# Audio attention: the weighted averages head by head in 32-column tiles of the tensor engine, and the four heads of a window picked by one ACT operation

## The chip, the cores and the metric

The program runs on one core of a Trainium2 chip. The metric is the device time of one execution in microseconds; lower is better. Times are medians over runs; rows of a trace come from one profiled execution. The engines are called PE (TensorE products), PEld (TensorE weight loads), DVE (VectorE), ACT (ScalarE), POOL (GpSimd) and SP (SyncE, whose queue issues the DMAs).

## The reference, cut to what matters

Two layers of cross attention and an MLP work on x (8 batches x 56 queries x 256), and then a second block lets the same queries attend to the 1500 rows of "audio". The change lies in that second block:

```python
B, Tt, D = hidden_states.shape        # 8, 56, 256; 16 heads of 16 columns
a = _layer_norm(audio_kv, ln_gamma, ln_beta)            # 8 x 1500 x 256
Q = (hidden_states @ Wq.T).reshape(B, Tt, HEADS, HEAD_DIM).transpose(0, 2, 1, 3)
K = (a @ Wk.T).reshape(B, Ta, HEADS, HEAD_DIM).transpose(0, 2, 1, 3)
V = (a @ Wv.T).reshape(B, Ta, HEADS, HEAD_DIM).transpose(0, 2, 1, 3)
scores = jnp.einsum('bhtd,bhsd->bhts', Q, K) * scale    # masked
attn = jax.nn.softmax(scores, axis=-1)
out = jnp.einsum('bhts,bhsd->bhtd', attn, V)            # the averages
out = out.transpose(0, 2, 1, 3).reshape(B, Tt, D) @ Wo.T
return hidden_states + jnp.tanh(gate) * out
```

## The kernel before, in words

Everything is f16 in two parts: a number is a high part plus a low part, and a product of two such numbers is two or three f16 products. A program of five queues without barriers, one for each engine, runs through the layers; semaphores are its only order.

**The two layers and the MLP** take the first 1147 us. The change doesn't touch them.

**The audio attention** works on tiles of 128 rows. For one batch the 16 heads x 56 queries are 896 rows, seven tiles (RT = 7), 56 tiles in all, numbered y; b is the batch and s the tile in it. Heads stand in four windows of four (HW = 4, NW = 4); a window is WR = 224 rows. Each head has 2 x 16 = 32 columns in the values, the high and the low half side by side (2 * KA = 32), so a window is 128 columns wide. For one tile:

- PE `audio_scores` forms 128 x 1536 scores in three banks of PSUM, 6 products where the tile touches one window and 12 where it touches two; it waits until DVE has read the scores of the tile before (`as_max`), since there is one set of banks.
- DVE `audio_minimum` (L1538) adds the mask and finds the extreme; ACT `audio_exponentiate` (L1286) takes the exponential; DVE `audio_scale` (L1545, L1547) forms the inverse sum; ACT `audio_high` (L1295) writes the high part of the probabilities, DVE `audio_low` (L1556) the low part.
- SP `turn_audio` (L555, L557) transposes high and low part by DMA into `probT`, 24 pieces (2 x NT, NT = 12) of up to 128 audio rows each.
- Between them PE forms `unit`s, the values and keys of the next batch (twelve a batch, 6 products of 512 columns each), which ACT (L1279) and DVE (L1597) split into high and low part, and SP (L546) transposes the keys.

**The averages.** Four times a batch PE runs `audio_average(b, w)` for a window: for high and low part of the probabilities, over 12 pieces of the audio rows, it loads 128 columns of values (four heads) and streams the window's 224 rows of `probT`. The bank then holds, for each head's 32 partitions, all four heads' queries, of which only the diagonal blocks of 32 x 56 are wanted. ACT `pick_average` takes these with four activations (L1303), adds a bias and writes `attnT`. PE may not overwrite the bank before that (`attn_ready`, two averages back).

The order is written out by hand: `SLOT_WINDOWS` says at which tile PE runs which window's average (tiles 1, 2, 4 and 6 of a batch; the last two windows in the batch after), `SLOT_PICKS` at which tile ACT picks it (0, 2, 3 and 5), `SLOT_UNITS` where the units stand. In PE's order a tile is: scores, one unit, an average if there is one, another unit. In ACT's: the high part of the tile before, units, a pick if there is one, the exponential. The last batch has no units. At the very end the last two windows of batch 7 are averaged, picked, multiplied with the output weights (f32, 56 columns, L769 SC<-small,ctxT) and written out.

L769 is the helper `mm` through which every product goes; groups of it are told apart by their tiles: SC<-qc are audio scores, SC<-ctxT units, PV<-core with 224 columns the averages of the change.

Of the kernel before, what the change touches and what calls it, by code (L numbers as in the profile page):

```python
# [18 lines left out]
ACT = mybir.ActivationFunctionType  # L19
# [6 lines left out]
B, Q, D, T, H, F = 8, 56, 256, 1500, 16, 1024  # L26
# [5 lines left out]
NT = -(-T // P)  # L32
# [11 lines left out]
KA = D // H  # L44
HW = 4
NW = H // HW
WR = HW * Q
# [15 lines left out]
PROB_SCALE = 4096.0  # L63
# [31 lines left out]
def build(nc, x_t, ctx_nat, ctx_t, ctx_p, mask, pack, vrows, gate, wq, wk, wv, wo, wkv2, wq2, wo2, w1, w2, scratch, out):  # L95
    es = ExitStack()
    with es:
        def sb(name, shape, dt=F32):
            return es.enter_context(nc.sbuf_tensor(name, shape, dt))

        def sem(name):
            return es.enter_context(nc.semaphore(name))
# [40 lines left out]
        probT = arena.bitcast(F16).rearrange("p (x r) -> p x r", x=2 * NT)  # L143
# [69 lines left out]
        attnT = small[:, 0:NW * NQ].rearrange("p (w n) -> p w n", w=NW)  # L213
        hm = sb("hm", [P, HW])
        vbias = sb("vbias", [P, NW])
# [5 lines left out]
        PV = [es.enter_context(nc.psum_tensor(f"PV{i}", [P, 512], F32)) for i in range(2)]  # L221
# [31 lines left out]
        attn_ready = sem("attn_ready")  # L253
# [168 lines left out]
        def values(n, w):  # L422

            v = n % VSLOTS * UNIT
            return core16[:, v + w * P:v + (w + 1) * P]
# [5 lines left out]
        def col(name, c):  # L431
            a = PACK[name] + c
            return pk[:, a:a + 1]
# [13 lines left out]
        def width(c):  # L447

            return LAST if c == NT - 1 else P
# [317 lines left out]
        def _(pe):  # L767
            def mm(o, a, c, start, stop, skip=False):
                return nc.tensor.matmul(o, a, c, start=start, stop=stop, skip_group_check=skip)  # L769
# [223 lines left out]
            def audio_average(b, w):  # L993

                n = NW * b + w
                y = RT * b + FIRST_TILE[w]
                if n >= 2:
                    pe.wait_ge(attn_ready, n - 1)
                if w == 0:
                    pe.wait_ge(m_lo, NT * (b + 1))  # L1000
                for i in range(2):
                    for k in range(2):
                        pe.wait_ge((apth_full, aptl_full)[i][k], 16 * ((y + 2 - k) // 2))
                    for j in range(NT):
                        r = width(j)
                        ins = mm(PV[w % 2][:, 0:WR], values(NT * b + j, w)[0:r, :],
                                 probT[0:r, i * NT + j, w * WR:(w + 1) * WR], j == 0 and i == 0, j == NT - 1 and i == 1)
                ins.then_inc(apv_done, 1)

            def audio_attention():  # L1010

                for y in range(RT * B + 3):
                    if y < RT * B:
                        audio_scores(y)
                    for n in slot_units(y)[0:1]:
                        unit(n, y)
                    if at_slot(SLOT_WINDOWS, y):
                        audio_average(*at_slot(SLOT_WINDOWS, y))
                    for n in slot_units(y)[1:]:
                        unit(n, y)  # L1020
                    if y == RT * B:
                        for m in range(DC):
                            early_output(m)
# [124 lines left out]
            for w in range(NW):  # L1148
                for c in range(DC):
                    pe.wait_ge(x_ready, 2 * DC + c + 1)  # L1150
                    ins = mm(banks[w][:, 0:NQ], wqa[:, c, w, :], xT[:, c, :], c == 0, c == DC - 1)
# [3 lines left out]
            for w in range(NW):  # L1155
                pe.wait_ge(attn_ready, NW * (B - 1) + w + 1)
                for m in range(DC):
                    ins = mm((M, S[0])[m][:, 0:Q], woa[:, w, m * P:(m + 1) * P], attnT[:, w, EARLY:NQ], w == 0, w == NW - 1)
# [5 lines left out]
        def _(act):  # L1164
# [132 lines left out]
            def pick_average(b, w):  # L1297

                n = NW * b + w
                act.wait_ge(apv_done, n + 1)  # L1300
                for h in range(HW):
                    own = slice(2 * KA * h, 2 * KA * (h + 1))
                    ins = nc.scalar.activation(attnT[own, w, b * Q:(b + 1) * Q], PV[w % 2][own, h * Q:(h + 1) * Q],  # L1303
                                               ACT.Identity, scale=1.0 / PROB_SCALE, bias=vbias[own, w:w + 1])
                ins.then_inc(attn_ready, 1)

            def mask_row(b, par):

# [10 lines left out]
            def audio_attention():  # L1319

                for y in range(RT * B + 4):
                    b, s = divmod(y, RT)
                    if 0 < y <= RT * B:
                        audio_high(y - 1)
                    for n in slot_units(y - 1)[1:]:
                        unit_high(n, y)
                    if at_slot(SLOT_PICKS, y):
                        pick_average(*at_slot(SLOT_PICKS, y))
                    if b < B:
                        audio_exponentiate(y)  # L1330
                    for n in slot_units(y)[0:1]:
                        unit_high(n, y)
                    if s == 3 and b + 1 < B:
                        mask_row(b + 1, (b + 1) % 2)
                    if s == 5 and b + 1 < B:
                        mask_addend(b + 1, (b + 1) % 2)
# [43 lines left out]
            for f in range(FC):  # L1380
                act.wait_ge(f1_mm, f + 1)
                if f >= 2:
                    act.wait_ge(f1_lo, f - 1)
                nc.scalar.activation(hid[:, f % 2, :], TB[f % 2][:, 0:NQ], ACT.Gelu, scale=1.0 / W_SCALE,
                                     bias=col("b_fc1", f)).then_inc(f1_act, 1)
# [473 lines left out]
```

## Time and profile before

| | |
|---|---|
| median of 3 runs | 1471.31 us (1470.87 to 1472.1) |
| the profiled execution: its time, its span | 1475.24 us, 1473.2 us |
| busy share: PE, PEld, DVE, ACT, POOL | 96%, 61%, 67%, 59%, 32% |
| instructions | 24729 |
| averages of the audio attention | 32, of 24 products of 224 columns |
| picks | 32, of 4 activations of 32x56 |

The span runs from the first to the last instruction; the execution's own time is a little longer. Busy time of products counts from the start of one to its modelled end, and products overlap, so two neighbouring starts say more than a mean duration. The chain that ended last is followed back from the last instruction, at each step to what released it.

### The profile page before, as it was taken

What the parts mean: (1) busy time and instruction counts of PE and PEld (TensorE: products, weight loads), DVE (VectorE), ACT (ScalarE), POOL (GpSimd) and SP (SyncE); (2) the same over time, 40 slices, a digit from 0 to 9 for tenths busy, and PEclk for the clock granted to TensorE, in tenths of its full rate; (3) what the DMA queues carried; (4) which work ended last, traced back from release to release, by engine and by line L of the source; (5) the groups of instructions that cost most, each with busy time, mean ns of one, the idle gap of its engine ahead of it and who ended that gap; (6) DMA issues with size and microseconds to landing.
All of it is one profiled execution on the core that took longest, in us unless ns stands there. A gap on an engine that the chain in (4) does not pass through costs nothing.

```text
span 1473.2 us, 24729 instructions
## 1 busy us (share of the span) xinstructions
PE 1417.8 (96%) x9188; PEld 891.8 (61%) x9188; DVE 985.8 (67%) x2034; ACT 868.5 (59%) x1566; POOL 471.0 (32%) x379
## 2 busy tenths in 40 slices
PE   9999999999999899999999999999999999999987
PEld 5466666666666554466666666666554454555545
DVE  6765555555555557766666566665556888888886
ACT  5744554455445447555445544554445788889896
POOL 3545334334334200234432523420011333334300
PEclk9999999999999999999999999999999999999999
DMA  6299899888888730599989989887722799999998
GB/s 207 78 227 192 164 183 184 175 173 179 179 172 182 150 97 29 115 207 182 190 161 185 182 165 181 179 165 147 180 51 50 136 210 211 220 214 223 215 199 164
DMA packets 672083, 246.95 MB, mean 168 GB/s; under 512 B 644716, under 2 KB 646236, under 8 KB 671964
## 3 DMA queue, kind: packets, MB, share of 16 engines
q1 hardware_dynamic: 671964, 245.38, 82.4%
q8 instruction: 73, 1.20, 0.4%
q14 instruction: 46, 0.38, 0.1%
HBM read 85.28 MB, written 0.52 MB: 58 GB/s over the span
## 4 chain that ended last, share of the span: by engine, by line
PE 71%; DVE 9%; ACT 7%; DMA 6%; issue 3%; SPq 2%; ACTq 0%; DVEq 0%
PE SC L769 38%; PE PV L769 33%; DMA core<-qc 3%; DVE qc L1556 2%; ACT qc L1295 2%; DVE core L1597 2%; DMA core<-core 2%; DVE prob L1538 2%; DMA qc<-core 2%; ACT prob L1286 1%; ACT core L1279 1%; ACT small L1303 1%; DVE core L1589 1%; SPq L515 1%; SPq L557 0%
## 5 line engine op out<-in xcount | busy, mean ns | idle before, releaser
L769 PE MATMUL PV<-core 128*128 128x256 f16 (+1 forms) x4800 | 540.5, 270 | 17.3 <-DMA core<-qc 5.6
L769 PEld LDWEIGHTS PV<-core 128*128 128x128 f16 x4800 | 458.4, 98 | 87.5 <-issue 13.7
L1228 ACT ACTIVATE prob<-SC,core 128x500 f32<-128x500 f32 x336 | 223.7, 674 | 413.0 <-DVE core L1562 413.0
L769 PE MATMUL SC<-ctxT,qc 128*128 128x500 f16 x2016 | 443.7, 374 | 0.0
L1531 DVE TENSOR_REDUCE mx<-SC 128x1 f32<-128x500 f32 x336 | 224.4, 669 | 322.5 <-PE SC L769 322.5
L769 PEld LDWEIGHTS SC<-ctxT,qc 128*128 128x128 f16 x2016 | 196.0, 97 | 206.8
L697 POOL CAST ctxT<-stage 128x750 f16<-128x750 f32 x64 | 68.9, 1076 | 446.7 <-PE SC L769 235.5
L1589 DVE SCALAR_TENSOR_TENSOR core<-prob,core 128x1500 f16<-128x1500 f32 x112 | 194.6, 1738 | 4.1 <-ACT core L1237 4.0
L1237 ACT ACTIVATE core<-prob 128x1500 f16<-128x1500 f32 x112 | 162.7, 1453 | 3.5
L769 PE MATMUL SC<-ctxT 128*128 128x512 f16 x576 | 136.9, 381 | 9.1 <-DVE core L1597 8.9
L769 PE MATMUL SC<-qc 128*128 128x512 f16 x480 | 112.7, 379 | 13.0 <-DVE mx L1538 13.0
L701 POOL TENSOR_TENSOR core<-stage,core 128x768 f16<-128x768 f32 x64 | 110.9, 1733 | 9.8 <-DVE core L1437 4.8
L701 POOL TENSOR_TENSOR ctxT<-stage,ctxT 128x750 f16<-128x750 f32 x64 | 102.6, 1604 | 12.8 <-DVE core L1437 8.0
L1556 DVE SCALAR_TENSOR_TENSOR qc<-prob,rsc,qc 128x1500 f16<-128x1500 f32 x56 | 100.2, 1788 | 9.2 <-ACT qc L1295 9.0
L769 PEld LDWEIGHTS SC<-ctxT 128*128 128x128 f16 x576 | 55.5, 98 | 77.2 <-DVE core L1597 12.4
L1538 DVE CUSTOM_DVE_ANT_0 prob<-SC,rowbuf 128x1500 f32<-128x1500 f32 x56 | 95.9, 1712 | 9.1 <-PE SC L769 9.1
L1295 ACT ACTIVATE qc<-prob,rsc 128x1500 f16<-128x1500 f32 x56 | 86.2, 1540 | 22.3 <-DMA core<-qc 14.0
L719 POOL CAST ctxT<-stage 128x768 f16<-128x768 f32 x32 | 26.8, 839 | 219.6 <-PE SC L769 147.9
L697 POOL CAST core<-stage 128x768 f16<-128x768 f32 x64 | 55.1, 860 | 130.6 <-DMA stage<-in_ctx_nat_dram 129.1
L1597 DVE SCALAR_TENSOR_TENSOR core<-SC,rstd,core 128x256 f16<-128x256 f32 x192 | 83.5, 477 | 19.3 <-ACT core L1279 19.2
L1286 ACT ACTIVATE prob<-prob,mx 128x1500 f32<-128x1500 f32 x56 | 86.4, 1544 | 13.7 <-DVE mx L1538 12.9
L769 PEld LDWEIGHTS SC<-qc 128*128 128x128 f16 x480 | 45.8, 97 | 68.8 <-issue 18.7
(134 smaller groups left out, 1329.0 us busy)
## 6 DMA issues: line engine op xcount, KB each, us to landing
stage<-in_ctx_nat_dram SPq DMA_DIRECT2D x64, 384.0 KB, 4.0
stage<-in_ctx_t_dram SPq DMA_DIRECT2D x64, 375.0 KB, 3.4
stage<-in_ctx_p_dram SPq DMA_DIRECT2D x32, 384.0 KB, 3.9
core<-in_wq_dram SPq DMA_DIRECT2D x8, 512.0 KB, 4.0
core<-in_wk_dram SPq DMA_DIRECT2D x8, 512.0 KB, 3.6
core<-in_wv_dram SPq DMA_DIRECT2D x8, 512.0 KB, 5.2
core<-in_wo_dram SPq DMA_DIRECT2D x8, 512.0 KB, 5.0
core<-core SPq DMA_TRANSPOSE x224, 4.2
```

The lines of the kernel that those rows point to most:

```text
L697: nc.gpsimd.tensor_copy(hi, src).then_inc(split_hi, 1)
L701: nc.gpsimd.tensor_tensor(lo, src, hi, ALU.subtract).then_inc(stage_free, 1)
L769: return nc.tensor.matmul(o, a, c, start=start, stop=stop, skip_group_check=skip)
L1228: nc.scalar.activation(prob[:, i, c * CW:c * CW + w], SETS[i][c][:, 0:w], ACT.Exp, bias=nmax[:, i, :], accum_out=sum3[:, i, c:c + 1]).then ...
L1237: nc.scalar.activation(ph[:, i, 0:T], prob[:, i, 0:T], ACT.Copy, scale=UP).then_inc(ph_hi, 1)
L1286: nc.scalar.activation(prob[:, i, 0:T], prob[:, i, 0:T], ACT.Exp, scale=-1.0, bias=mx3[:, i, 0:1], accum_out=sum3[:, i, 0:1]).then_inc(as_ ...
L1295: nc.scalar.activation(aph[:, i, 0:T], prob[:, i, 0:T], ACT.Copy, scale=rsc[:, y % 4, 1:2]).then_inc(aph_hi, 1)
L1531: nc.vector.tensor_reduce(mx3[:, t % 2, c:c + 1], SETS[t % 2][c][:, 0:w], AX_X, ALU.max)\
L1538: nc.vector.tensor_tensor_reduce(out=prob[:, i, 0:T], in0=scores_of(y), in1=maskb[:, b % 2, :], scale=1.0, scalar=3.0e38, op0=ALU.add, op1 ...
L1556: nc.vector.scalar_tensor_tensor(aph[:, i, TC:TC + T], prob[:, i, 0:T], rsc[:, y % 4, 1:2], aph[:, i, 0:T], ALU.mult, ALU.subtract).then_i ...
L1589: nc.vector.scalar_tensor_tensor(ph[:, i, TC:TC + T], prob[:, i, 0:T], UP, ph[:, i, 0:T], ALU.mult, ALU.subtract).then_inc(ph_lo, 1)
L1597: ins = nc.vector.scalar_tensor_tensor(lo[:, i, :, :], src[:, i, :, :], rstd[:, n:n + 1], hi[:, i, :, :], ALU.mult, ALU.subtract)
```

## The change

Each of the 24 steps of an average becomes four: for head h the 32 columns of its values are loaded, the 56 rows of its own queries are streamed, and the result goes to the head's own 32 partitions of the bank, in columns 0 to 55. An average is then 96 loads of 32 columns and 96 products of 56 columns. The bank holds the wanted blocks only, side by side in the partitions, so ACT picks a window with one activation of 128x56.

```diff
                     for j in range(NT):
                         r = width(j)
-                        ins = mm(PV[w % 2][:, 0:WR], values(NT * b + j, w)[0:r, :],
-                                 probT[0:r, i * NT + j, w * WR:(w + 1) * WR], j == 0 and i == 0, j == NT - 1 and i == 1)
+                        v = values(NT * b + j, w)
+                        for h in range(HW):
+                            own = slice(2 * KA * h, 2 * KA * (h + 1))
+                            c = w * WR + h * Q
+                            ins = mm(PV[w % 2][own, 0:Q], v[0:r, own], probT[0:r, i * NT + j, c:c + Q],
+                                     j == 0 and i == 0, j == NT - 1 and i == 1)
                 ins.then_inc(apv_done, 1)
...
                 act.wait_ge(apv_done, n + 1)
-                for h in range(HW):
-                    own = slice(2 * KA * h, 2 * KA * (h + 1))
-                    ins = nc.scalar.activation(attnT[own, w, b * Q:(b + 1) * Q], PV[w % 2][own, h * Q:(h + 1) * Q],
-                                               ACT.Identity, scale=1.0 / PROB_SCALE, bias=vbias[own, w:w + 1])
-                ins.then_inc(attn_ready, 1)
+                nc.scalar.activation(attnT[:, w, b * Q:(b + 1) * Q], PV[w % 2][:, 0:Q], ACT.Identity,
+                                     scale=1.0 / PROB_SCALE, bias=vbias[:, w:w + 1]).then_inc(attn_ready, 1)
```

## Rows read from the trace of the kernel before

**Rows 1.** The page: the chain that ended last, by engine.
```profile
PE 71%; DVE 9%; ACT 7%; DMA 6%; issue 3%; SPq 2%; ACTq 0%; DVEq 0%
```

**Rows 2.** The chain by line, cut to 1184.4 to 1426 us, then to 1426 to 1473.2.
```profile
by line: DMA core<-qc 15.9%; issue 12.7%; DVE qc L1556 10.0%; DMA qc<-core 9.7%; ACT qc L1295 9.0%; PE SC L769 7.6%; DVE core L1597 6.4%; ACT core L1279 5.2%; ACT prob L1286 5.1%; DVE prob L1538 5.1%; PE PV L769 3.5%; ACT small L1303 3.2%; 
...
by line: ACT qc L1295 12.9%; DVE qc L1556 11.1%; ACT prob L1286 10.5%; PE SC L769 9.5%; SPq L557 9.4%; issue 9.0%; DMA core<-qc 8.7%; SPq L555 6.8%; ACT small L1303 6.5%; DVE prob L1538 5.1%; PE PV L769 2.8%; DVE rsc L1545 1.5%; DVE rsc L15
```

**Rows 3.** us of the stretch, busy PE, PEld, DVE, ACT, POOL; PE clock, DMA share, GB/s.
```profile
1184.40:1225.80 41.40, 38.58 (x230) 21.62 (x229) 35.78 (x64) 36.13 (x53) 15.44 (x12) 1.00 1.09 214
...
1348.60:1390.00 41.40, 38.82 (x230) 21.70 (x229) 36.98 (x66) 37.41 (x55) 15.43 (x12) 1.00 1.13 214
```

**Rows 4.** Timeline of PE: start, us, what, count; a batch in its middle.
```profile
1277.30 1.46 PE L769 MATMUL SC<-qc 128*128 128x512 f16 x6
1278.59 1.46 PE L769 MATMUL SC<-ctxT 128*128 128x512 f16 x6
1279.89 2.47 PE L769 MATMUL PV<-core 128*128 128x224 f16 x24
1282.20 1.03 PE L769 MATMUL SC<-ctxT 128*128 128x512 f16 x4
```

**Rows 5.** Waits, 1184.4 to 1390 us: total us, times, longest.
```profile
ACT qc L1295 <- DMA core<-qc: 12.5, 8, 2.7
...
DVE prob L1538 <- PE SC L769: 6.7, 9, 1.8
...
PE PV L769 <- issue: 4.1, 3, 2.0
```

**Rows 6.** The chain in order of time, first pieces of two picks.
```profile
1439.09 0.30 ACT small L1303
...
1443.97 0.30 ACT small L1303
```

**Rows 7.** Groups by shape on ACT, by name: the pick and its neighbours in size.
```profile
L1303 ACT ACTIVATE small<-PV,vbias x128: 282/298/303, 1175.4 to 1469.7; 32x56 f32<-32x56 f32 x128
...
L1209 ACT ACTIVATE small<-SC x2: 532/532/532, 60.7 to 600.7; 32x448 f16<-32x448 f32 x2
...
L1342 ACT ACTIVATE small<-small x2: 558/558/558, 508.0 to 1047.5; 128x448 f16<-128x448 f32 x2
```

**Rows 8.** Timelines of PE and PEld where products are small.
```profile
308.85 0.17 PE L769 MATMUL SC<-one,rowbuf 128*128 128x1 f16 x1
308.88 4.09 PE L769 MATMUL PV<-core 128*128 128x256 f16 x36
...
1086.73 1.84 PE L769 MATMUL SC<-pk,prob 128*128 128x1 f32 x16
1088.43 0.92 PE L769 MATMUL PV<-prob,core 128*128 128x448 f16 x4
...
1468.49 1.42 PEld L769 LDWEIGHTS SC<-small,ctxT 128*128 128x128 f32 x12
```

**Rows 9.** Timeline of PE where the width changes to 32 and back.
```profile
25.82 1.30 PE L769 MATMUL SC<-prob,core 128*128 128x448 f16 x6
26.95 1.30 PE L769 MATMUL SC<-core 128*128 128x448 f16 x6
28.18 0.93 PE L769 MATMUL SC<-prob,core 128*32 128x448 f16 x4
29.04 1.31 PE L769 MATMUL PV<-prob,core 128*128 128x448 f16 x6
```

**Rows 10.** Timeline of the last 20 us.
```profile
1453.70 1.46 PE L769 MATMUL SC<-qc 128*128 128x512 f16 x6 [1.91 <-DVE mx L1538]
...
1467.44 1.31 PE L769 MATMUL PV<-core 128*128 128x224 f16 x12 [0.48 <-DMA core<-qc]
...
1468.59 2.13 PE L769 MATMUL SC<-small,ctxT 128*128 128x56 f32 x16
1468.79 1.23 ACT L1303 ACTIVATE small<-PV,vbias 32x56 f32<-32x56 f32 x4 [2.47 <-PE PV L769]
```

## The prediction

> **What bounds the kernel now.** I read the page first: the tensor engine is busy 96% of the span (the table above) and holds 71% of the chain that ended last [rows 1]. That is an average over stages, so the second view is the chain cut to the stage that the change touches, the audio attention from about 1147 us on. There TensorE no longer leads: between 1184 and 1426 us its lines hold 7.6% and 3.5% of the chain, the DMA transposes 15.9% and 9.7%, DVE and ACT most of the rest [rows 2]. The third view, busy time by batch, shows why: in a batch of seven tiles TensorE is busy some 93% of the time, DVE and ACT 86 to 90%, DMA all of it, and the granted clock is 1.00 of 2.4 GHz [rows 3]. Busy is not occupied for TensorE, so I count: a batch issues 60 + 72 products of 512 columns, six of which take 1.29 us (1277.30 to 1278.59), and four averages of 2.31 us (1279.89 to 1282.20) [rows 4]. That is 132 x 0.215 + 4 x 2.31 = 37.6 us, against a mean batch of 41.1 us (five batches from 1184.4 to 1390.0, the first and the last in [rows 3]). TensorE has 3.5 us of room in a batch, 0.88 us for each average. The waits say where that room lies: in front of the averages (4.1 us of "issue", which I take for transposes still under way), while ACT waits 12.5 us for the same transposes to free its buffer [rows 5]. Last I read the stretch without units of keys and values (1426 us on): there ACT holds the chain, with three whole picks of four activations (1430.5, 1439.1, 1444.0), and L1303 alone has 6.5% [rows 2, 6].
>
> **The change, part by part.**
>
> The pick. Four activations of 32x56 take 1.23 us together, 0.30 us each [rows 7, 10]. One activation of 128x56 stands nowhere in the trace. From the nearest rows, 32x448 takes 532 ns and 128x448 558 ns, so four times the partitions cost at most 26 ns [rows 7]; I take 0.31 us, with 0.30 and 0.33 as ends. 32 picks save 0.92 us each: 29 us of ACT, most of it not on the chain.
>
> The average. 24 loads of 128 columns with products of 224 columns become 96 loads of 32 columns with products of 56: the same columns stream, in four times as many instructions. Before, 24 pairs take 2.31 us, 96 ns a pair, and the weight load is hidden behind the product. After, the product needs 96/4 = 24 ns, so whatever a small pair costs beside that decides. No row has such a pair. From below: if nothing else limited, 24 ns. From above: if a pair keeps today's pace whatever its size, 96 ns. Nearest rows: a product of one column is followed by the next pair after 0.03 us (308.85 to 308.88), so one pair can pass in 30 ns [rows 8]; sixteen loads of 128 f32 columns, each with a product of one column, take 1.70 us, 106 ns each, so 32 columns at that rate load in 26.5 ns; twelve such loads with 56-column products take (1.42 - 0.19)/11 = 112 ns each, so load and product overlap even when the product is short [rows 8]. I take 28 ns a pair, between 26.5 and 30: 96 x 0.028 = 2.69 us.
>
> To this comes the change of the array's shape. The trace has it: six full products of 448 columns take 1.13 us to the next group, but 1.23 us when the next group is 32 columns wide, and the four narrow ones then take 0.86 us to the next full one where 4 x 0.188 = 0.75 us would do [rows 9]. That is 0.10 us in and 0.11 us out, 0.21 us for each average. Its two halves have the same shape, so nothing is lost between them. Sum: 2.69 + 0.21 = 2.90 us against 2.31, +0.59 us an average, +2.4 us a batch. TensorE then needs 40.0 of 41.1 us: it still fits, barely.
>
> What it comes to. Between 1184 and 1426 us L1303 is 3.2% of a chain of 241.6 us, 7.7 us; a quarter of it remains, so 5.8 us go at most. Other chains run close beside it (DVE, transposes), so I count half, -2.9 us. The averages are 3.5%, 8.5 us; a quarter more is +2.1 us at first order, and 28 x 0.59 = 16 us if every average before the last batch's were on the path [rows 2]. In the last batch TensorE idles some 2 us before its scores [rows 10], so a longer average hides there, while the three picks on the chain give 3 x 0.92 = 2.8 us, of which I keep 2.3, since the transposes queued on SP from 1455 us on follow ACT only in part [rows 2, 6]. The end: the last half average starts at 1467.44, when its transpose lands, and takes twelve pairs, 1.15 us; 48 x 0.028 = 1.34 us plus the shape change in front of the closing products make +0.2 us, and the last pick gives -0.92 us, with the output products behind it [rows 10]. Sum: -2.9 + 2.1 - 2.3 - 0.7 = -3.8 us.
>
> The profiled execution took 1475.2 us for a span of 1473.2, 3.9 us above the median of 1471.3. A difference read in it is taken off the median: 1467.5 us. Without the cover named for the averages it is +14 us instead of +2.1, which is 1479 us.
>
> No DMA, no wait and no order on any queue changes, and ACT reads the same values from the bank as before. The instructions grow by 32 x 2 x 72 = 4608; against 24729 now, which I cost at nothing: the loads of a batch's averages are spread over 41 us.
>
> **The rivals.**
>
> *The four column tiles work at once.* Each head's weights sit in their own 32 columns; if a load and a product in one tile need not wait for those in the next, four pairs pass in 28 ns, 7 ns a pair, 0.67 + 0.21 = 0.9 us an average; half-way, at 14 ns, 1.6 us. TensorE gives 0.7 to 1.4 us back four times a batch. For it: nothing in the rows speaks against; the narrow products there all use one tile [rows 9]. Against: every load in the rows waits for its turn behind the one before. The chain's 8.5 us of averages shrink by 0.3 to 0.6 of them, -2.6 to -5 us in place of +2.1. With -2.9, -2.3 and -0.9 from the picks that is -10 us; DVE waits 6.7 us for scores in five batches [rows 5], of which I let 2 go: 1459 us, ends 1451 and 1465.
> The Trainium skill, TensorEngine Tiling (Array Packing), Key Properties, states that different tiles can load and multiply in parallel; by it this rival is the outcome. No row here has two tiles, so it is not shown.
>
> *A small pair costs more than 31 ns* (the other side). From 0.88 us of room, (2.31 + 0.88 - 0.21)/96 = 31 ns is where TensorE becomes the bound of every batch. If a load into a narrow tile does not overlap with the product before it, the pair is 26.5 + 24 = 50 ns, an average 5.0 us, +2.7 us, +10.8 us a batch: TensorE needs 48.4 us, with 1 us of waits 49.4, 8.3 us more than now, over about seven batches +58 us, less 5 us for the picks: 1525 us. At 35 ns it is about 1484 us; at today's 96 ns, 9.4 us an average, it would be some 180 us. For it: the 56-column pairs in the rows were never quicker than 112 ns, though of four times the columns and another type. Against: the 30 ns of one pair.
> The Trainium skill, TensorE: Matmul & The Clock Gate, Back-to-back issue gap, gives about 62 ns a MATMUL when it is decoded in microcode, and about 25 ns as the floor otherwise; by the first an average is 6.2 us and the time near 1555 us, by the second my 28 ns stand. The pair of 30 ns speaks for the second, but it is one pair and not ninety-six.
>
> *Nothing moves*: the DMA transposes (25.6% of the chain) pace the batches, and ACT's relief turns into waiting for them. Time: the end alone gives -3.0 us, the averages give that back: 1471 us. For it: that share, and ACT's 12.5 us of waits for them [rows 2, 5]. Against: the picks in the last batch, which no transpose covers [rows 6].
>
> **How the numbers follow.** A measurement of this kernel tells a change from none beyond 0.2%, 2.9 us. Serial pairs of 24 to 31 ns, my case: 0.34, at 1467.5 us, range 1460 to 1478; of it 0.23 is faster, 0.05 same, 0.06 slower. Nothing moves: 0.07, at 1471, all of it same. Tiles at once: 0.32, at 1459; 0.30 faster, 0.02 same. Dear pairs: 0.27, at 1525, from 1476 up; 0.26 slower, 0.01 same. Together faster 0.53, same 0.15, slower 0.32. The range reaches down to 1453 (0.05 lies below) and up to 1500, which takes in pairs up to some 40 ns and leaves 0.14 above.
>
> **What would show it.** PV<-core with 128x56 products, x3072 in place of 768; the 96 of one average, start to start, take 2.7 us plus 0.2: about 1.6 or 0.9 means tiles at once, 5 dear pairs. The pick as one activation of 128x56, x32, near 0.30 us. A batch still 40 to 42 us, with ACT down to some 80%. In the last stretch, picks follow one another at 4.0 us where it was 4.9 (1439.1 to 1444.0) [rows 6]. The granted clock stays full. I am wrong if the pair is over 31 ns, if the clock falls in the averages, or if the batches shorten by more than 1.5 us.

## The result, and the profile after

The changed kernel takes 1483.2 us (1481.2 to 1483.9, four runs); the kernel before took 1471.7 beside it. The ratio is 1.0071, 95% interval 1.0056 to 1.0086: 0.7% slower, where I had forecast 0.25% faster. It lies inside the range, on the wrong side.

The parts that the change names came out better than my central case. First the timeline of PE around one average, the pick, and the shapes of the averages (groups by shape, whole trace), against [rows 4, 7]:

```profile
1272.52 1.46 PE L769 MATMUL SC<-ctxT 128*128 128x512 f16 x6
1273.91 1.02 PE L769 MATMUL PV<-core 128*32 128x56 f16 x96
1275.22 1.46 PE L769 MATMUL SC<-qc 128*128 128x512 f16 x6 [0.28 <-DVE mx L1539]
```
```profile
L1305 ACT ACTIVATE small<-PV,vbias x32: 286/288/307, 1172.5 to 1475.5; 128x56 f32<-128x56 f32 x32
```
```profile
L769 PE MATMUL PV<-core 128*32 128x56 f16 x2816 | 34.0, 194 | 42.7 <-DMA core<-qc 31.9 <-issue 8.9 <-DVE core L1598 1.7
```

96 pairs of load and product take 1.02 us, 10.6 ns a pair, where 24 pairs took 2.31 us. (The 1.02 us hold the 0.19 us of the last product; from start to start a pair takes 8.3 ns.) The 56 columns of one product alone need 24 ns by the pace of the wide ones, so the four tiles do work at once. The four activations became one of 0.29 us. TensorE and ACT should have gained. But PE now stands idle 42.7 us before its averages, 31.9 of them for the DMA transposes of the probabilities. Before, the same row was

```profile
L769 PE MATMUL PV<-core 128*128 128x224 f16 x704 | 77.5, 261 | 9.8 <-DMA core<-qc 5.6 <-issue 4.1
```

The windows of five batches (same columns as [rows 3]; each from the first tile's minimum to the next batch's) say what that adds up to:

```profile
1183.00:1225.80 42.80, 35.05 (x518) 16.61 (x517) 35.88 (x64) 32.31 (x41) 15.44 (x12) 0.96 1.16 212
...
1352.00:1399.30 47.30, 35.66 (x518) 16.78 (x517) 36.00 (x63) 34.70 (x43) 15.42 (x12) 0.93 1.14 203
sum 216.30, PE 175.19 PEld 82.66 DVE 179.14 ACT 163.91 POOL 77.17; mean PE 35.04 PEld 16.53 DVE 35.83 ACT 32.78 POOL 15.43
```

PE's busy time of a batch fell from 38.6 to 35.0 us and ACT's from some 36 to 32.8, and yet the five batches take 216.3 us in place of 205.6. (The batch behind them took 34.4 us in place of 37.3, so 2.9 us of these 10.7 came back.) The DMA share stays at its full value. The whole stage, from the first minimum on DVE to the last, before and then after (xcount, shortest/median/longest, first and last start):

```profile
L1538 DVE CUSTOM_DVE_ANT_0 prob<-SC,rowbuf x56: 1707/1710/1721, 1148.9 to 1455.7; 128x1500 f32<-128x1500 f32 x56
```
```profile
L1539 DVE CUSTOM_DVE_ANT_0 prob<-SC,rowbuf x56: 1706/1710/1722, 1146.0 to 1460.5; 128x1500 f32<-128x1500 f32 x56
```

That is 306.8 us before and 314.5 after: 7.7 us lost in the stage. From the last minimum to the end of the span it is 17.5 us and 20.8: 3.3 us more. Together 11.0 of the 11.5 us. (The two spans differ by 8.1 us only, because the stage began 2.9 us earlier in the trace after. The layers in front of it are untouched, and in the traces of the experiments it begins anywhere from 1145.1 to 1149.0 us, whichever averages the kernel has; only e9's begins later.)

The waits from 1184.4 to 1397 us answer to [rows 5], the chain by line to [rows 2] (1184.4 to 1426 us, then 1426 to the end):

```profile
ACT qc L1299 <- DMA core<-qc: 30.4, 16, 2.9
PEld PV L769 <- issue: 28.6, 25, 2.6
PE PV L769 <- DMA core<-qc: 23.0, 18, 3.5
```
```profile
by line: DMA core<-qc 25.2%; DMA qc<-core 10.6%; DVE qc L1557 9.4%; PE SC L769 9.0%; issue 8.3%; ACT qc L1299 7.1%; SPq L555 4.6%; SPq L557 4.3%; DVE core L1598 4.0%; DVE prob L1539 3.4%; ACT core L1283 3.3%; ACT prob L1290 2.5%; SPq L485 1
...
by line: SPq L555 38.0%; SPq L557 27.1%; DMA core<-qc 9.3%; PE SC L769 6.5%; issue 4.9%; DVE prob L1539 3.1%; ACT qc L1299 2.6%; ACT rowbuf L1317 2.6%; PE PV L769 1.4%; ACT prob L1290 1.1%; DVE xT L1675 0.5%; SPq L554 0.3%; DVE mx L1539 0.0
```

The transposes' share of the chain grew from 25.6 to 35.8%, and in the last batch the chain runs on SP's queue, from one issue of a transpose to the next. So the transposes pace the stage, and they became slower. The DMA view of 1184 to 1430 us shows that, before and after (packets, MB and busy share per queue: q1 carries the data, q8 TensorE's instructions, q14 GpSimd's; last, a transpose's median us from issue to landing):

```profile
DMA packets 176670, 52.64 MB, mean 214 GB/s; under 512 B 173323, under 2 KB 174091, under 8 KB 176651
...
q1 hardware_dynamic: 176651, 52.40, 112.4%
q8 instruction: 11, 0.18, 0.4%
...
core<-qc SPq DMA_TRANSPOSE x87, 4.1
```
```profile
DMA packets 169727, 51.11 MB, mean 208 GB/s; under 512 B 166367, under 2 KB 167135, under 8 KB 169695
...
q1 hardware_dynamic: 169695, 50.65, 115.3%
q8 instruction: 24, 0.39, 0.6%
...
core<-qc SPq DMA_TRANSPOSE x83, 4.9
```

Only one line counts more work: q8, blocks of 16 KB of instructions, 24 in place of 11. The 4608 instructions that the change adds are, by the page's own blocks (91 against 73, 1.49 MB against 1.20), 18 blocks more. Those hardly count by their bytes. They count by what happens around them. The same view over 4 us around one such block, before (1225 to 1229 us) and after (1210 to 1214), in 40 slices of 0.1 us:

```profile
DMA  9999999999999999999999000000000100000399
GB/s 225 212 207 207 205 228 212 215 218 174 141 174 182 241 259 412 220 218 187 105 20 3 0 0 0 0 0 0 0 5 8 10 8 10 10 10 8 77 292 289
```
```profile
DMA  9999999999999999190000001000005999999999
GB/s 154 174 246 287 294 289 289 292 292 292 267 287 282 435 276 154 36 20 0 0 0 0 3 8 10 8 10 10 10 10 113 284 292 297 289 289 289 294 292 500
```

For 1.7 and 1.4 us all data traffic of the core stops; 8 to 10 GB/s is the block itself. It is the same in both kernels, only over twice as often after. Counted from the packets of 1190 to 1420 us, stretches of at least 0.4 us under 60 GB/s add up to 16.6 us before and 34.3 after; 10.9 and 29.4 us of that lie at q8 blocks. After, 20 of the 22 blocks of this stretch have such a stop (before, 7 of 10); it lasts 1.0 to 2.0 us, median 1.4, and begins some 0.4 us behind the block's first packet. Part is caught up: behind the stop the queue moves some 290 GB/s.

The transposes feel it one by one. From 1184 to 1430 us, those that had a q8 block in flight between their issue and their landing landed after a median of 5.5 us before (23 of them) and 5.6 after (35); those that had none landed after 4.1 us in both kernels (63 and 26; the trace records no landing for the rest), and none of these took over 5.2 us. So a single transpose is not slower for the change; more of them meet a block.

Could TensorE instead be waiting for its own instructions? After, its idle stretches of over 0.2 us from 1184 to 1430 us add up to 45.2 us; 0.5 us of it ended while a block was being fetched or within 0.6 us behind it. Of the 8.7 us that PE waits for "issue" before averages, 8.1 end within 0.25 us of a transpose's landing.

At the end the granted clock is the other thing that changed. Two windows of after, the second from the closing products on, and PE's last row, against [rows 10]:

```profile
1470.00:1475.40 5.40, 2.11 (x145) 1.79 (x144) 0.00 (x0) 0.31 (x1) 0.00 (x0) 0.50 1.08 191
1475.40:1481.30 5.90, 3.64 (x20) 3.46 (x16) 0.55 (x2) 0.31 (x1) 0.00 (x0) 0.50 0.05 10
```
```profile
1475.37 3.66 PE L769 MATMUL SC<-small,ctxT 128*128 128x56 f32 x16
```

The closing products run at a granted clock of 0.50, the 1.2 GHz level, 3.66 us where 2.13 stood; TensorE had waited for the last transposes before them.

### The profile page after: what moved, and what is told of

It is laid out like the page before. It is cut to its first block, busy times and chain, and to the rows that moved or that the text cites. A ratio compares the mean times of both kernels' runs of the same rounds, so it can differ in the third digit from the quotient of the medians.

```text
span 1481.3 us, 29241 instructions
## 1 busy us (share of the span) xinstructions
PE 1386.8 (94%) x11492; PEld 850.4 (57%) x11492; DVE 983.5 (66%) x2034; ACT 837.3 (57%) x1470; POOL 472.1 (32%) x379
## 3 DMA queue, kind: packets, MB, share of 16 engines
q8 instruction: 91, 1.49, 0.4%
## 4 chain that ended last, share of the span: by engine, by line
PE 71%; DMA 8%; DVE 8%; SPq 6%; ACT 5%; issue 2%; ACTq 0%; DVEq 0%
PE SC L769 38%; PE PV L769 32%; DMA core<-qc 5%; SPq L555 2%; DVE qc L1557 2%; DMA qc<-core 2%; SPq L557 2%; DMA core<-core 2%; ACT qc L1299 1%; DVE core L1598 1%; DVE prob L1539 1%; ACT core L1283 1%; ACT prob L1290 1%; DVE core L1590 1%; SPq L485 1%
## 5 line engine op out<-in xcount | busy, mean ns | idle before, releaser
L769 PE MATMUL PV<-core 128*128 128x256 f16 (+1 forms) x7104 | 494.5, 238 | 49.8 <-DMA core<-qc 31.9
L769 PEld LDWEIGHTS PV<-core 128*128 128x128 f16 (+1 forms) x7104 | 415.6, 97 | 124.6 <-issue 40.2
L769 PE MATMUL SC<-ctxT 128*128 128x512 f16 x576 | 140.9, 389 | 9.2 <-DVE core L1598 9.1
L769 PE MATMUL SC<-qc 128*128 128x512 f16 x480 | 118.1, 391 | 20.1 <-DVE mx L1539 17.3
L1557 DVE SCALAR_TENSOR_TENSOR qc<-prob,rsc,qc 128x1500 f16<-128x1500 f32 x56 | 100.2, 1788 | 16.2 <-ACT qc L1299 11.0
L701 POOL TENSOR_TENSOR ctxT<-stage,ctxT 128x750 f16<-128x750 f32 x64 | 102.6, 1604 | 12.8 <-DVE core L1438 8.0
L769 PEld LDWEIGHTS SC<-qc 128*128 128x128 f16 x480 | 46.0, 100 | 81.9 <-issue 36.5
```

The lines of the kernel that those rows point to most:

```text
L701: nc.gpsimd.tensor_tensor(lo, src, hi, ALU.subtract).then_inc(stage_free, 1)
L1557: nc.vector.scalar_tensor_tensor(aph[:, i, TC:TC + T], prob[:, i, 0:T], rsc[:, y % 4, 1:2], aph[:, i, 0:T], ALU.mult, ALU.subtract).then_i ...
```

## The experiments

Theories named in the expectations: A, the transposes pace the stage, so what ACT or TensorE saves turns into waits; B, the loss is the clock that falls when TensorE idles between its shorter averages; C, it is TensorE coming early, so that its units and scores press on the other queues. From e5 on: F, the fetched blocks of TensorE instructions; G and G', the tiles themselves, or the SBUF reads of their loads, disturb the DMA engines; H is C again. Ratios are to the kernel before, run beside the experiment. "Blocks" are q8 blocks from 1184 to 1430 us, 11 before and 24 after. Where work is left out, the expectation says which.

**e1, tiles alone.** The pick with four activations, as before, on the new layout:

```python
for h in range(HW):
    own = slice(2 * KA * h, 2 * KA * (h + 1))
    ins = nc.scalar.activation(attnT[own, w, b * Q:(b + 1) * Q], PV[w % 2][own, 0:Q], ...)
```

> The averages as 32-column tiles, but each window still picked by four ACT operations of 32x56. Theory A (the queue of DMA transposes on SP sets the pace of the audio stage, so that what ACT or TensorE saves turns into waits): the time is that of the changed kernel, 1481 to 1486 us, since ACT's 0.93 us a pick were on no path. Rival (ACT's relief gives something and the tiles cost all of it): 1486 to 1500 us, as 32 x 0.93 = 30 us of ACT work come back.

1485.3 us, 1.0086 (1.0069 to 1.0102), 23 blocks from 1184 to 1430 us. The whole loss comes with the tiles.

**e2, the pick alone.** The averages as before, one activation of 128x56.

> The averages as before (128 columns, 224 rows), each window picked by one ACT operation of 128x56; it takes the first head's queries for all four heads, so three quarters of the picked values are others than the reference's. Theory A: 1469 to 1472 us, at most the three picks on the chain of the last batch (2.8 us) are gained. My prediction's step (half of the picks' 3.2% of the chain is gained): 1465 us. Rival (a faster ACT crowds the transposes and costs time by itself): 1474 us or more.

1469.6 us, 0.9981 (0.997 to 0.9992): 29 us less of ACT buy 2.8 us, 1.2 to 4.4 by the interval.

**e3 and e4, TensorE filled.** In front of each average's wait, twelve products of 224 columns (e3, the clock), or five f32 products of one column, which hold TensorE up without streaming (e4, the early start):

```diff
+                for j in range(12):
+                    mm(PV[w % 2][:, 256:256 + WR], values(NT * b + j, w), core16[...][:, 0:WR], True, True)
```
```diff
+                for _ in range(5):
+                    mm(PV[w % 2][:, 256:257], dmean[:, :], dmean[:, 0:1], True, True)
```

> The changed kernel, and in front of each average, before its wait for the transposes, 12 further full products of 224 columns (1.15 us), whose result nobody reads: TensorE is as long busy as before the change. Theory B (the loss comes from TensorE's granted clock, which falls in 1.2 GHz stretches where the shorter averages leave the array waiting): granted clock back to 0.99, time 1470 to 1474 us. Theory C (the loss comes from pacing: an earlier TensorE makes the transposes meet and slows them): also 1470 to 1474 us; the next run tells them apart. Neither: 1483 us or more.

> The changed kernel, and in the same place five f32 products of one column (ten weight loads of 106 ns, 1.06 us), whose result nobody reads: TensorE is as long occupied as before the change but streams next to nothing. Theory B (the clock): the clock stays at 0.98 to 0.985 and the time at 1481 to 1487 us. Theory C (pacing): the pace of before is back, 1470 to 1475 us, whatever the clock.

e3: 1482.0 us, 1.0064 (1.005 to 1.0079), mean clock 0.992 in place of 0.985, closing products at full clock again (1.99 us), loss nearly unchanged. e4: 1486.5 us, 1.0087 (1.0071 to 1.0103). B and C fall as causes of the main loss. e3's ratio is 1 us below that of the change, which these intervals can't tell from nothing; in the traces its end, from the last minimum on, is 3.6 us shorter (17.2 us for 20.8).

**e5, a quarter of the products; e6, the same with one-column products in the other places; e13, those with one-column loads too.** All three have the tiles, the order and the waits of the changed kernel. In e5, `for h in range(HW) if j + i == 0 else (j % HW,)` leaves 27 of 96 products. In e6:

```diff
+                            n = Q if j + i == 0 or h == j % HW else 1
+                            ins = mm(PV[w % 2][own, 0:n], v[0:r, own], probT[0:r, i * NT + j, c:c + n], ...)
```

and in e13 also `own = slice(own.start, own.start + 1)` where n is 1.

> The changed kernel with about a quarter of each average's products: for piece j only head j mod 4 (27 products of 56 columns in an average in place of 96; the other heads' averages are left out, so values are wrong). Tiles, picks and waits stay. TensorE then has about the instruction count of the kernel before. Theory F (the 4608 added TensorE instructions are fetched over the same DMA engines, 18 more blocks of 16 KB, in a stage that the DMA transposes pace, and slow them): the loss is gone, 1473 us or below. Theory G (the four tiles at once, reading SBUF fast, hinder the DMA transposes): also mostly gone, about 1475, since the reading is a quarter. Theory H (a TensorE that is ready earlier lets more work pile onto the one DMA queue, whatever its instructions): as slow as the changed kernel or slower, 1483 to 1488.

> The same as the quarter, but the 69 products of an average that it left out stand there with one column in place of 56 (values of the other heads wrong). Instructions, tiles and order are those of the changed kernel; the columns read are a quarter. F: as slow as the changed kernel, about 1483. G: as the quarter without them, about 1475 or below. H: as slow as the changed kernel.

> The quarter with one-column products, whose 69 filling products of an average now also load one column of weights in place of 32 (values of three heads in four wrong, as there). TensorE's instructions are those of the changed kernel, the SBUF reads of the loads and of the columns a third or less. Theory F (fetched blocks): 1481 to 1485, as the changed kernel. Theory G' (the reads of the loads disturb the DMA engines): 1474 to 1477, as the quarter.

e5: 1476.2 us, 1.0017 (1.0004 to 1.0029), 12 blocks. e6: 1483.4 us, 1.0071 (1.0058 to 1.0083), 24 blocks. e13: 1484.2 us, 1.0073 (1.006 to 1.0085), 23 blocks. Three quarters of the streamed columns make no difference, nor do the loads' reads; 69 nearly empty instruction pairs an average do, all of it. G, G' and H fall. Of e5's 2.5 us up to 1.5 are its closing products, 3.66 us long as after (that row of its trace starts at 1468.50).

**e7, two heads a tile**: 48 products of 112 columns an average, picked by four activations.

> Averages as two tiles of 64 columns, two heads each: 48 products of 112 columns in an average, picked by four ACT operations. Added TensorE instructions 1536 in place of 4608, 6 more fetched blocks in place of 18. F: a third of the loss, about 1477. G: near the full loss (the same columns in about the same time), about 1482. H: about 1480 to 1484.

1478.4 us, 1.0047 (1.0033 to 1.0062), 15 blocks. A middle dose gives a middle loss, though more than F's third.

**e8, instructions on GpSimd.** 90 waits on a semaphore long reached behind each of 52 instructions of GpSimd in the stage.

> The kernel before, with 4680 instructions more on GpSimd in the audio stage (52 groups of 90 waits on a semaphore that has long been reached; they touch no memory). TensorE's program is untouched. F: these too are fetched over the DMA engines, so a loss like that of the change, 1478 to 1484. G and H: no change, 1473, unless GpSimd's own work comes late.

1473.3 us, 1.0005 (0.9994 to 1.0016): nothing. The DMA view shows why this is no test of TensorE's blocks:

```profile
q8 instruction: 11, 0.18, 0.3%
q14 instruction: 24, 0.20, 0.2%
```

GpSimd's come by another queue in blocks of 8 KB, 16 more, and a transpose that met one of them (and none of q8) landed after 4.3 us, one that met neither after 4.15. Averaged over the 24, the rate fell for about 0.5 us and nothing was missing 4 us later; averaged over 115 blocks of q8 in five kernels with tiles (the changed one, e1, e3, e4 and e6), the traffic of 1.1 us was missing 2 us later and that of 0.3 us still after 4. My expectation F was wrong here; what it says is borne out for TensorE's blocks alone.

**e9, waits on TensorE.** Eight waits before each 512-column product, no tiles.

> The kernel before, with some 4500 instructions more on TensorE in the audio stage that touch no memory: eight waits on a semaphore long reached before each 512-column product of the scores and of the audio units (two waits make one instruction, so four more for each of some 1100 products; at 17 ns each by the SyncE queue's rows they fit beside a product of over 200 ns). No tiles. Theory F (each block of TensorE instructions that is fetched, 16 KB on queue q8, stops the other DMA traffic for about a microsecond, in a stage that the DMA transposes pace): about the loss of the change, 1479 to 1485, with some 18 more blocks. Theory G' (the 32-column weight loads and the tiles disturb the DMA engines' access to SBUF): no loss, 1473.

1656.1 us, 1.124. It tells nothing of fetching: a wait on TensorE is dear. Six products with their waits, second row, take 2.46 us from start to start (1301.66 to 1304.12), and without them 1.29 [rows 4]:

```profile
1300.12 1.46 PE L769 MATMUL SC<-qc 128*128 128x512 f16 x6
1301.66 2.62 PE L769 MATMUL SC<-ctxT 128*128 128x512 f16 x6
1304.12 2.47 PE L769 MATMUL PV<-core 128*128 128x224 f16 x24
```

**e14, halved products**, which replaces e9: the kernel before, each 512-column product of scores and units as two of 256 with the same weights:

```diff
+                for half in (slice(0, 256), slice(256, 512)):
+                    ins = mm(unit_bank(n, y)[:, half], ctxA[...], wkv[:, wi, d, half], ...)
```

> The kernel before, with each 512-column product of the audio scores and units made as two of 256 columns with the same weights, and no tiles: some 1100 pairs more (2200 instructions, 8 or 9 blocks of 16 KB). F: half the change's loss, 1.003 to 1.005, 1476 to 1480, and more if TensorE's busy time of a batch (38.6 us of 41.4 before) grows by over 2 us. G': no change unless that busy time grows so.

1478.5 us, 1.0035 (1.0019 to 1.005), 17 blocks, a transpose lands after 4.3 us. TensorE's busy time, over windows as long as the five batches before (205.6 us), is what it was, 38.5 us a batch for 38.7:

```profile
sum 205.60, PE 192.53 PEld 172.18 DVE 177.06 ACT 180.68 POOL 77.15; mean PE 38.51 PEld 34.44 DVE 35.41 ACT 36.14 POOL 15.43
```
```profile
q8 instruction: 17, 0.28, 0.4%
...
core<-qc SPq DMA_TRANSPOSE x86, 4.3
```

The same products, no tiles, nearly half the added instructions: half the loss. One thing besides the count changed: the weights are loaded twice as often (PEld 34.4 us a batch for 21.9). e6 and e13 speak against the loads, but for tiles only. The closing products ran at full clock (2.13 us), so the clock at the end has no part in it. (The profiled execution took 1475.0 us, below the median; the ratio is over all runs.)

**e11 and e12, without the low transposes.** Before and after, each without the transposes of L557:

```diff
-                sp.dma_start_transpose(probT[:, NT:2 * NT, s * P:(s + 1) * P], aph[:, i, TC:2 * TC])\
-                    .then_inc(aptl_full[i], 16)
```

> The kernel before without the DMA transposes of the low halves (the low products read the high half again, so the averages' low part is wrong; 56 of the stage's transposes are gone). If the transposes pace the stage, it falls to what TensorE needs: its 38.6 us busy of a batch of 41.4, so 1450 to 1463.

> The changed kernel without the same transposes. F: with the DMA queue relieved the blocks that are fetched hold up nothing that paces, and the tiles save what they take off TensorE (32 averages by about 1.1 us): 20 to 35 us faster than the kernel before without those transposes. G' or any loss that tiles bring to TensorE itself: no more than 10 us faster.

e11: 1460.0 us, 0.9916 (0.9899 to 0.9932). e12: 1444.5 us, 0.9808 (0.979 to 0.9826). Against each other the tiles are 15.6 us faster here, though they fetch 28 blocks from 1184 to 1430 us against 11:

```profile
q1 hardware_dynamic: 111936, 36.16, 77.8%
```
```profile
q1 hardware_dynamic: 117173, 37.48, 83.3%
q8 instruction: 28, 0.46, 0.8%
...
core<-qc SPq DMA_TRANSPOSE x49, 4.1
```

The share is 83% where the changed kernel had 115%, and the chain of e12 from 1184 to 1400 us no longer has a transpose in front:

```profile
by line: DVE prob L1536 27.1%; DVE qc L1552 24.0%; DVE core L1593 23.7%; issue 8.8%; ACT rowbuf L1314 4.2%; ACT qc L1296 4.0%; ACT core L1280 2.6%; DVE rsc L1545 1.8%; ACT prob L1287 1.2%; DVE rsc L1543 1.1%; DVE anym L1611 0.5%; DVE anym L
```

Each of the five batches takes 38.7 us in e11, where PE leads the chain (SC 36.2%, PV 12.8%), and 36.5 us in e12. The gain is less than F's 20 to 35 us; DVE, with three quarters of e12's chain, has taken over as the bound. A block now costs a transpose little: with one in flight it lands after 4.3 us in e12, without after 4.0.

**e10, tiles for the last two averages alone; e15, with filling.** `if n < NW * B - 2:` keeps the old products and picks for all others. e15 adds 28 products of 224 columns before the last average.

> The kernel before, with tiles and the single pick for the last two averages alone (windows 2 and 3 of the last batch), whose average and pick stand on the chain at the end. 288 instructions more. F: one block more at most, so the loss of the change is gone, and the two averages (1.1 us shorter each) and the last pick (0.9 us shorter) give back up to 3 us: 1469 to 1472. G': much the same, since few products are tiles.

> The kernel with tiles for the last two averages alone, with 28 products of 224 columns (whose result nobody reads) before the last average, in TensorE's idle 3.0 us there. If the granted clock of 0.50 after that idle time cost the end, the closing 16 products take 2.1 us in place of 3.7 and the time falls by 1.5 to 2.5 us to 1471 to 1473, level with the kernel before or up to 0.1% below it. If not, it stays at 1474.

e10: 1474.2 us, 1.0012 (1.0003 to 1.0021), no gain, with two blocks more in the whole execution (75 for 73) and none in 1184 to 1430 us. Its last rows on PE:

```profile
1463.84 0.75 PE L769 MATMUL PV<-core 128*32 128x56 f16 x48 [3.02 <-DMA core<-qc]
1465.09 0.75 PE L769 MATMUL PV<-core 128*32 128x56 f16 x48 [0.50 <-DMA core<-qc]
1465.77 3.66 PE L769 MATMUL SC<-small,ctxT 128*128 128x56 f32 x16
```

and those of e15:

```profile
1463.48 0.54 PE L769 MATMUL PV<-core 128*32 128x56 f16 x48 [0.18 <-DMA core<-qc]
1464.76 0.54 PE L769 MATMUL PV<-core 128*32 128x56 f16 x48 [0.73 <-DMA core<-qc]
1465.23 1.99 PE L769 MATMUL SC<-small,ctxT 128*128 128x56 f32 x16
```

e15: 1472.6 us, 0.9995 (0.9984 to 1.0006), 1.6 us below e10 by the medians and 2.5 by the ratios, as expected, though the two intervals overlap a little. The rows show where it comes from: quick tiles left TensorE idle for 3.0 us, the clock fell to 0.50, and the closing products paid for it, 3.66 us for 1.99. It is level with the kernel before, no better. No version with the right results beat the kernel before by more than a measurement tells.

**All traces together.** The length of the stage, read as above from the first minimum to the last, follows the blocks. Each is one execution, so a step of 2 us means little:

| kernels | blocks | stage, us |
|---|---|---|
| before, e2, e8, e10, e15 | 11 | 304.2 to 306.9 |
| e5 | 12 | 307.6 |
| e7 | 15 | 310.4 |
| e14 | 17 | 308.7 |
| after, e1, e3, e4, e6, e13 | 23 to 26 | 311.6 to 316.8 |

In all of them a transpose with a q8 block in flight lands after a median of 5.0 to 5.9 us, and one without after 4.1 to 4.2.

## Why the prediction was wrong

**The step that failed** is the sentence "The instructions grow by 32 x 2 x 72 = 4608; against 24729 now, which I cost at nothing". I asked only whether TensorE could issue them in time. They are fetched over the DMA engines, 18 blocks of 16 KB, nearly each of them stops the data traffic for over a microsecond, and in this stage the DMA engines were full (a share of 1.09 to 1.13 in [rows 3]). e6 and e13 show that the added instructions, whatever they do, carry the loss; e14 that this needs no tiles; e11 and e12 that it becomes a gain where the transposes don't pace. That the stop at a block is how the one leads to the other rests on the traces (the landings with and without a block, the stage by number of blocks) and on these sizes: 13 blocks more, 0.3 us each still missing 4 us later and up to 1.1 us for a transpose that something waits for, make 4 to 14 us around the 7.7 lost in the stage. No run changed the fetching alone, so how the loss divides among the blocks stays open, and so does why e7 lost 6.9 us for 1536 instructions where e14 lost 5.2 for 2112.

**What paces.** I read "DMA all of it" and a chain with 25.6% of transposes, and then gave the rival in which the transposes pace the batches 7 in 100. That rival had the right mechanism and stopped half-way: it let relief come to nothing, and never asked what else the change puts on the resource that paces.

**The average.** "I take 28 ns a pair" was the wrong case of three: 8.3 ns from start to start, 1.02 us of products, and 1.03 us from the average's start to the next group (1273.91 to 1275.22, less 0.28 of wait), against 2.90 foreseen. Where nothing had to be waited for it is 0.93 us (e12, 1175.97 to 1176.90). The change of shape costs 0.10 us on the way in, as foreseen (1272.52 to 1273.91 is 1.39 us, for the usual 1.29). The rival "tiles at once" named this almost to the number, 7 ns a pair and 0.9 us an average, and gave 1459 us; its first half came true, its time missed by 24 us, by the same step: it too costed the instructions at nothing. (The 16 us of averages without cover, 28 x 0.59, stand as +14 in the forecast's next paragraph; nothing hangs on it.) The Trainium skill, TensorEngine Tiling (Array Packing), Key Properties, states that different tiles can load and multiply in parallel; the trace agrees.

**Dear pairs.** Excluded by the same row: a pair took 8.3 ns, so neither the 62 ns nor the 25 ns quoted with this rival held for pairs in four tiles. The kernel became slower, as this rival says, but not by its mechanism.

**The pick.** 0.31 us was right (0.288). "-2.9", "-2.3" and "-0.7" together are 5.9 us; e2 measured 2.8 for all three.

**The last batch and the end.** Picks no longer lead there, but SP's queue does, which a row of before held already (16.2% of the chain for L555 and L557) [rows 2]. The "-0.7" for the end became +3.3: the last transpose was issued 1.4 us later behind the last minimum (8.88 us for 7.44) and landed after 5.13 us for 4.11; the rest from the closing products on took 1.3 us more at the lower clock (the products alone 1.5), less 0.5 us for the quicker half average. "The granted clock stays full" was wrong: 0.93 to 0.96 in four of five batches (one of five before), 0.50 at the end. By e3 and e15 only the end's part costs anything, 1 to 2.5 us by their ratios, which are hardly clear of noise; the closing products themselves show 1.5 to 1.7.

**The room in a batch.** "TensorE then needs 40.0 of 41.1 us: it still fits, barely" was the wrong worry; at 35.0 us busy it had more room than before, and none of it reached the end.

## What to carry to other kernels

Where the DMA engines are full in every slice, count a change's instructions as DMA work: look at the instruction queue in the DMA view, divide the added instructions by what a block holds (4608 made 18 blocks here, 256 each), and look at what the rate does around one block and at how long the transfers take that meet one. A change that makes one engine quicker by issuing four small instructions for one belongs where DMA has room; here the same edit lost 0.7% in a full stage and won 1.1% where a third of the traffic had been taken out. And when an engine gets quicker just before the end, see what clock its last products then run at.

## What the runs showed of the hardware that was not expected

- In this stage a fetched block of TensorE instructions (16 KB, taking 1.0 to 1.3 us on average) stopped all other DMA traffic of the core for a median of 1.4 us at 20 of 22 blocks after and 7 of 10 before: from some 210 GB/s to none but its own 8 to 10, then some 290 to catch up. A transpose in flight then landed after 5.5 us for 4.1. A GpSimd block (8 KB) slowed the traffic for about 0.5 us, and the transpose landed after 4.3 us.
- Four column tiles of 32 take a pair of load and 56-column product every 8.3 ns from start to start (96 in 1.02 us with the last one's end).
- At the lower clock a half average of 48 such pairs took 0.75 us in place of 0.54 (e10, e15), and the f32 products 3.66 in place of 1.99.
- Waits in TensorE's program cost: four wait instructions (eight waits) before each product of 512 columns took six products from 1.29 to 2.46 us (e9).
